# Causal attention over eight sequences: where the value products stand in TensorE's hand-written program

## The reference

```python
qkv = jnp.einsum('btd,de->bte', x, w_qkv).reshape(B, T, 3, h, Hd)
...
logits = jnp.einsum('bhqd,bhkd->bhqk', q, k) * scale
mask = jnp.tril(jnp.ones((T, T), dtype=x.dtype))
logits = logits + (1.0 - mask)[None, None, :, :] * big_neg
attn = jax.nn.softmax(logits, axis=-1)
out = jnp.einsum('bhqk,bhkd->bhqd', attn, v)
```

## Time and profile before

| | |
|---|---|
| median of 3 executions | 4616.25 us (4610.25 to 4618.79) |
| the profiled execution | 4618.48 us, of which 4616.8 us span |
| busy share of the span | TensorE 87%, its weight loads 55%, VectorE 66%, ScalarE 50%, GpSimd 51% |
| attention | about 835 to 1756 us of the span |
| granted clock within attention | 1.00 from 865 to 1698 us |

### The profile page before, as it was taken

How to read it: one execution, slowest core, us unless ns; L and a number is a source line. 1 busy time by engine, 2 the same in 40 slices (tenths; PEclk the granted TensorE clock), 3 DMA queues, 4 the chain that set the end, 5 groups by cost and what they waited for, 6 DMA issues and landing times. The chain is left out here.

```text
span 4616.8 us, 118840 instructions
## 1 busy us (share of the span) xinstructions
PE 4004.6 (87%) x49612; PEld 2548.5 (55%) x49612; DVE 3047.8 (66%) x5270; ACT 2330.9 (50%) x3872; POOL 2372.3 (51%) x1536
## 2 busy tenths in 40 slices
PE   4499798899999997459979799699999999997799
PEld 3366454233333334336647444387787778776577
DVE  6411154888888875631137477599899899997575
ACT  2122143577777772012226378667777776774233
POOL 1144434222222224124523265399999999998454
PEclk7699899899999998679989999899999999998899
DMA  7323366655555636233332466633333443342662
GB/s 213 110 47 50 74 216 218 95 94 94 94 94 94 94 62 219 90 101 51 52 75 74 142 241 245 216 90 97 99 95 94 102 100 94 96 102 81 248 226 82
DMA packets 339596, 549.37 MB, mean 119 GB/s; under 512 B 55488, under 2 KB 239200, under 8 KB 339040
## 3 DMA queue, kind: packets, MB, share of 16 engines
q1 hardware_dynamic: 285552, 467.46, 38.6%
q0 software_dynamic: 24576, 34.10, 4.6%
q10 hardware_dynamic: 28912, 40.02, 2.4%
HBM read 335.69 MB, written 212.32 MB: 119 GB/s over the span
## 5 line engine op out<-in xcount | busy, mean ns | idle before, releaser
L2532 POOL TENSOR_TENSOR s_hc<-s_hs,s_ct 128x1024 f32<-128x1024 f32 x512 | 1214.4, 2387 | 66.8 <-DVE s_hs L2511 51.5
L2511 DVE TENSOR_TENSOR_SCAN s_hs<-s_dA,s_psB 128x1024 f32<-128x1024 f32 x512 | 1169.0, 2286 | 100.2 <-POOL s_hc L2532 29.0
L2435 PE MATMUL s_psB<-s_diag,s_duT 128*32 128x128 f32 x32768 | 961.1, 274 | 80.0 <-DVE s_hs L2511 44.0
L2435 PEld LDWEIGHTS s_psB<-s_diag,s_duT 128*32 128x32 f32 x32768 | 909.0, 111 | 184.0 <-issue 102.4
L1382 DVE CUSTOM_DVE_ANT_0 a_masked<-a_psM,k_later 128x1024 f32<-128x1024 f32 (+7 forms) x1024 | 724.6, 750 | 146.7 <-PE a_psM L1440 144.2
L1364 ACT ACTIVATE a_wt<-a_psE 128x512 f32<-128x512 f32 (+1 forms) x1216 | 625.6, 578 | 268.3 <-PE a_psE L1466 258.9
L2376 ACT ACTIVATE s_dA<-s_dlt,s_aneg 128x1024 f32<-128x1024 f32 x512 | 587.6, 1148 | 341.2 <-DVE s_hs L2511 335.9
L1343 POOL TENSOR_SCALAR_AFFINE_SELECT a_wt<-a_wt 128x512 f32<-128x512 f32 x256 | 163.2, 637 | 692.9 <-ACT a_wt L1364 692.8
L2356 ACT ACTIVATE s_diag<-s_ident,s_bt 128x128 f32<-128x128 f32 x956 | 317.5, 388 | 13.4 <-ACT s_ys L2365 13.4
L1440 PE MATMUL a_psM<-a_kst,a_qst 96*128 96x512 bf16 (+3 forms) x1152 | 306.0, 330 | 14.4 <-DVE a_mx L1382 10.6
L1466 PE MATMUL a_psE<-a_qst,a_kst 99*128 99x512 bf16 (+3 forms) x1152 | 308.8, 329 | 7.6 <-ACT a_wt L1364 6.5
(11 more groups left out here) (366 smaller groups left out, 6236.0 us busy)
## 6 DMA issues: line engine op xcount, KB each, us to landing
s_dlt<-dd SPq DMA_DIRECT2D x128, 512.0 KB
a_qst<-qs SPq DMA_DIRECT2D x144, 128.0 KB
a_kst<-ks SPq DMA_DIRECT2D x144, 128.0 KB
yd<-s_ys ACTq DMA_DIRECT2D x33, 512.0 KB
vs<-a_va ACTq DMA_DIRECT2D x32, 512.0 KB, 3.6
zsd<-s_zs SPq DMA_DIRECT2D x32, 512.0 KB, 2.7
ucd<-s_uc SPq DMA_DIRECT2D x8, 2048.0 KB, 9.3
dd<-s_dl SPq DMA_DIRECT2D x32, 512.0 KB, 4.1
```

Source lines behind the costliest of these rows:

```text
L2435: ins = pe.matmul(psB[s][DG * m:DG * (m + 1), c * P:(c + 1) * P], duT[j % 2][:, c, DG * r:DG * (r + 1)], diag[:, place(NB * g + m, u), c, ...
L2511: dve.tensor_tensor_scan(hs[k % 2][:, :], dA[k % 2][:, :], psB[s][:, :], 0.0, ALU.mult, ALU.add).then_inc(scanned, 1)
L2532: pool.tensor_tensor(hc[NB * (g % 2) + r][:, :], hs[k % 2][:, :], ct[:, g, :], ALU.mult).then_inc(weighed, 1)
```

## The change

The value products of a unit are issued behind the first share of the unit two later, where they stood behind its third share of four, or its second share of two. Where the products are a half's first (values 0 and 4) they stay behind the last share, as before. In units with one share there is nothing to move. So eight of twelve calls a group move: values 10, 1, 2, 5, 6, 7, 8 and 9, in units 0, 3, 4, 7, 8, 9, 10 and 11. Nothing else in any engine's program changes.

```diff
                     for i in range(len(shares)):
                         score(k, i)
-                        if k >= LAG and i == (len(shares) // 2 if early else len(shares) - 1):
+                        if k >= LAG and i == (0 if early else len(shares) - 1):
                             values(k - LAG)
```

## The result

| | before | after |
|---|---|---|
| median | 4616.25 us (4610.25 to 4618.79) | 4662.77 us (4657.15 to 4666.02) |
| ratio, 95% interval | | 1.0099 (1.0085 to 1.0113) |
| span of the profiled execution | 4616.8 us | 4664.3 us |
| parts to parts, in most periods | 28.80 us | 30.02 us |
| first to last parts (31 periods) | 896.4 us | 936.3 us |

Each median is of three executions. Slower by 46.5 us, 39 to 52 by the interval, where 31.5 was forecast.

What follows compares the result with a forecast made beforehand. VectorE was taken to set 8.74 us of each 28.80 us period and TensorE 20.06. Terms of 0.90 + 0.21 + 0.53 - 1.09 + 0.43 + 0.07 gave +1.05 us a group, +31.5 over 30 periods: 4648 us, range 4622 to 4664.

Steps and rivals of the forecast that it cites:

- the narrower 4638 to 4660: The forecast's own range in us, each of five terms off by 0.1 to 0.2, ScalarE's bound on top.
- step 1: Values 5 and 6 delay TensorE's first 256-column tile and VectorE runs dry: +0.90 us a group.
- 2 to 5: Values 7, 8, 10, 1 and 2 at later tiles: +0.21, +0.53 with -1.09 in return, +0.43, +0.07 us a group.
- step 6: Costs taken as nothing, such as GpSimd's masking and ScalarE's closer shares, the latter bounded by 0.33 us a group.
- The count of periods: 31 periods between 32 parts; first and last counted as one, so 30 periods and +31.5 us.
- Faster, as the wait behind the parts is filled: Rival: values 6 and 7 stay covered, step 4 free; 0.56 us a group saved, 4599 us; chance 0.11.
- No change: Rival: VectorE's dry spell is half as long, sum within 0.3 us a group, 4616 to 4625 us; chance 0.11.
- Slower still: Rival: ScalarE's exponentials bind too, 0.33 us a group at two places at most, 4658 to 4668 us; within forecast's 0.78.
- The occupancy rule: Work on the engine of highest occupancy, here TensorE at 96%; a mere reordering would then give 0.

Runs made afterwards that it cites:

- u7_u8: Against the kernel before, only the value calls in units 7 and 8 (values 5 and 6) moved forward: 4651.54 us against 4616.94.
- u8: Against the kernel before, only the value call in unit 8 (values 6) moved forward: 4659.55 us against 4619.93.
- all_but_u7_u8: Against the kernel before, the value calls in units 0, 3, 4, 9, 10 and 11 moved forward: 4624.49 us against 4616.94.
- second series: The changed kernel measured once more beside the kernel before: 4660.92 us against 4619.93.
- u10: Against the kernel before, only the value call in unit 10 (values 8) moved forward: 4609.04 us against 4616.94.
- before_inv13: The kernel before with only VectorE's reciprocal moved, to behind the 14th tile of maxima: 4613.93 us against 4618.79.
- all_inv13: The changed kernel with the reciprocal behind the 14th tile of maxima instead of the 25th: 4642.73 us against 4616.94 for the kernel before.

## Why the prediction was right, and where it was short

**Sign, place and mechanism: right.** The size was short: 4662.77 us is 1.2 below the upper end of the stated 4622 to 4664, and above the narrower 4638 to 4660. Step by step, in us a group:

| step | forecast | measured |
|---|---|---|
| 1, VectorE dry before the first 256-column tile | +0.90 | +0.91 (u7_u8, u8) |
| 2 to 5, with values 8 gone from behind the third tile | +0.15 | +0.32 (all_but_u7_u8) |
| sum | +1.05 | +1.22 |

Parts came at 8.80 for 8.79, the third tile 1.60 behind them for 1.59. The ninth tile came 7.11 behind the third (1253.54 to 1260.65) for 7.00. VectorE's new idle time before the first 256-column tile was 0.77 where I had said about 0.85, that before the seventh tile 0.53 for some 0.5. The wait ahead of the ninth tile, forecast as about 0.4, is 0.27 in the record and 0.44 from start to start.

**The term that was mis-sized is step 6,** "I take zero, since the gaps just fit". They did not. Of the two shares at 1256.54, which have 0.44 us of work, the second starts late, at 1256.89; the next tile follows at 1257.10, 0.12 us late. ScalarE began the exponential of the share three before it at 1256.15:

```profile
1256.15 2.07 ACT L1364 ACTIVATE a_wt<-a_psE 128x512 f32<-128x512 f32 x4 [0.55 <-PE a_psE L1466]
```

With 0.60 for it and the 0.14 that the forecast took for the way back, the bank comes free at 1256.89, as measured. No run changed this wait alone. The forecast kept 0 to 0.33 for this and took the end that cost nothing. With it, the sum is 1.17 of the 1.22; the rest are hundredths at the joins.

**The count of periods was fair.** The 29 periods in the middle make 29 times 1.22, 35.4 us. The first one grew by 0.2 (31.72 to 31.90, though over all traces it lies anywhere from 29.7 to 34.5, so this number is chance), the last by 1.0 (27.55 to 28.56), and from the last parts to the last copy of `a_psO` it is 1.8 more: 31.9 us before (1723.8 to 1755.7), 33.7 after (1763.3 to 1797.0). For these ends, 3.0 us together, I had counted one period. With 3.3 us more of excess above the commonest period and the first parts 0.4 earlier, attention ends 41.3 us later in the trace (1755.7 to 1797.0).

**What was missed altogether** is the falls of the clock: I wrote of the granted clock as given, though the forecast itself made TensorE's waits longer. Over the kernel before, they are worth 0.1 and 3.3 us in the two traces of the change, and 8.6 in u8. The other 6 or so of the span's 47.5 us lie in the scan, three stages later: between the last product of `mamba_inputs` (L2174) and the first of `mamba_mix` (L2816) 1396.4 us passed before and 1403.2 after, 1396 to 1405 in the other kernels. None of these kernels touches that stage; I can't say more than that it varies by this much. From the first parts to the last copy of `a_psO` the two traces of the change take 41.7 and 36.3 us more than the kernel before. That what is left of the 46.5 is chance is suggested by the +41 of the second series, and not shown beyond it.

**The rivals.** "Faster, as the wait behind the parts is filled" had its mechanism right and is real in u10, at half its price. In the change it lost to step 1, by the very number named as deciding: VectorE's start on the first 256-column tile moved from 2.39 to 3.29 us behind the first one of 384 columns (1276.45, that tile being issued at 1273.16, one period after 1243.14). "No change" fell with it, and its own sum was off: with half of step 1's 0.90 the total is still +0.60 a group, 18 us, not within 0.3; step 1 would have had to shrink to 0.15. "Slower still" by ScalarE was right in kind, at one place and 0.12 us. The occupancy rule of the Trainium skill (Perfetto Trace Analysis, Identifying the Most-Contended Engine), taken alone and as the prediction read it, gave zero. TensorE's share of a period was 96% before and 92% after, with no less work done. The page's warning that matmul busy time is a bad measure is what this case bears out, though not for the page's reason that pipelined instructions look smaller: here the overlapping ends made TensorE look fuller, with 0.40 us of idle time in the record ahead of the third 1024-column tile and 0.56 by start times (0.16 more; the prediction has 0.17).

## What to carry to other kernels

Where two in-order engines feed each other through a few buffers, find in the timeline which one sets the time in which stretch, and put long work of the feeding engine where the other has its backlog, never just ahead of the other's longest unbroken stretch. A wait in the profile is a ceiling, not a price: filling it moves the late tile, and the next wait takes part of the gain back (half in u10, three quarters in before_inv13), so replay one period with start-to-start times. Here that gave periods to 0.1 us, but for the first forecast (0.17 short) and all_inv13 (0.4). And look for idle time in the trace of the kernel that you are going to edit, since the last edit may have moved it.

## What the runs showed of the hardware

TensorE's granted clock fell to the 1.2 GHz level (0.51 in its row) for 3.4 us after a stretch of 1.5 us in which TensorE had been busy for 0.79, most of the rest being the end of its new wait, though over a usual period it was busy for 92%; neighbouring periods with the same wait kept 1.00. In the four traces with that wait in each period there were 4, 1, 4 and 7 falls, all of them 0.9 to 2.1 us behind its end, and in the nine traces without it none in the same stretch. One kernel's two traces had 4 and 1. The four periods with a fall in the first trace of the change took 0.6 to 1.1 us more. So such a wait can cost more than its length, in some periods and not in most, and a single profile may hold 3 us more or less of it.
